# Attention with GpSimd additions of exponentials: block-4 masks placed before the last two additions, one addition in six on VectorE for half of the head groups, later deviations placed after the masks

## What is computed

```python
scores = jnp.einsum('bsnh,btnh->bnst', k, q) / math.sqrt(HEAD_SIZE)
scores = jnp.triu(scores) + -10000.0 * jnp.tril(ones, k=-1)
attn = jax.nn.softmax(scores, axis=2)
out = jnp.einsum('bnkq,bknh->bqnh', attn, v)
out = out.reshape(b, s, NUM_HEADS * HEAD_SIZE)
return out @ Wo + bo
```

## Time and profile before

| | us |
|---|---|
| median of 3 runs (lowest, highest) | 1638.31 (1636.98, 1640.26) |
| the profiled execution | 1638.2 |
| its span in the trace | 1636.3 |
| TensorE busy | 1543.4 |
| VectorE busy | 948.3 |
| ScalarE busy | 796.6 |
| GpSimd busy | 596.5 |
| mean granted share of the TensorE clock | 0.983 |

### The profile page before, as it was taken

One profiled execution on the slowest core, in us unless ns is written; L12 is line 12 of the kernel. 1 busy time (PEld: TensorE's weight loads), 2 busy tenths in 40 slices (PEclk: granted clock), 3 DMA queues, 4 the chain that ended last, 5 costly groups with the idle time before them and its releaser, 6 DMA issues.

```text
span 1636.3 us, 24454 instructions
## 1 busy us (share of the span) xinstructions
PE 1543.4 (94%) x9286; PEld 642.0 (39%) x9288; DVE 948.3 (58%) x1897; ACT 796.6 (49%) x1284; POOL 596.5 (36%) x812
## 2 busy tenths in 40 slices
PE   4899999999999999999998999999999999999997
PEld 2333333333433333343332344444444444444443
DVE  5657766689666878667876333554434343434344
ACT  5356666567666666755786743232222222222222
POOL 4335664677665667746765310020000000000001
PEclk9899999999999999999999999999999999999999
DMA  4221322114421233222355431221111111111000
GB/s 180 91 53 42 83 59 53 53 62 108 122 45 28 85 98 96 73 53 50 107 168 157 129 102 40 58 97 39 45 27 52 26 52 26 52 26 52 0 26 26
DMA packets 113398, 112.26 MB, mean 69 GB/s; under 512 B 69632, under 2 KB 69632, under 8 KB 113024
## 3 DMA queue, kind: packets, MB, share of 16 engines
q1 hardware_dynamic: 113280, 110.69, 24.0%
HBM read 45.37 MB, written 25.17 MB: 43 GB/s over the span
## 4 chain that ended last, share of the span: by engine, by line
PE 72%; POOL 14%; DVE 5%; issue 5%; ACT 3%; POOLq 0%; ACTq 0%; DVEq 0%
PE ps L968 27%; PE ps L889 15%; PE ps L985 13%; PE ps L952 10%; POOL pt L1459 7%; PE ps L926 4%; DVE mcol L1247 2%; POOL rs L1379 1%; PE ps L902 1%; POOL pt L1450 1%; POOL stage L1443 1%; POOL atl L1469 1%; PE ps L910 1%; POOL rs L1376 1%; ACT tq L1074 1%
## 5 line engine op out<-in xcount | busy, mean ns | idle before, releaser
L1101 ACT ACTIVATE pt<-ps,nrm 128x512 f32<-128x512 f32 (+1 forms) x640 | 360.7, 645 | 220.6 <-PE ps L926 202.7
L968 PE MATMUL ps<-x2in,gu 128*128 128x512 f16 x2048 | 462.4, 379 | 0.0
L1247 DVE TENSOR_REDUCE mcol<-ps 128x1 f32<-128x512 f32 (+2 forms) x600 | 305.7, 575 | 149.9 <-PE ps L910 76.6
L968 PEld LDWEIGHTS ps<-x2in,gu 128*128 128x128 f16 x2048 | 200.2, 98 | 241.9 <-ACT sg L1122 0.5
L1376 POOL TENSOR_SCALAR rs<-mv 128x1 f32<-128x1 f32 x120 | 29.9, 249 | 644.7 <-DVE mv L1146 638.2
L1318 DVE SCALAR_TENSOR_TENSOR hf<-ps,usc,sg 128x512 f32<-128x512 f32 x128 | 96.1, 751 | 259.3 <-PE ps L968 245.7
L1127 ACT ACTIVATE hh<-hf 128x512 f16<-128x512 f32 x128 | 80.7, 630 | 258.1 <-DVE hf L1318 244.5
L1459 POOL TENSOR_TENSOR pt<-pt 128x1024 f32<-128x1024 f32 x84 | 203.4, 2442 | 1.8 <-ACT pt L1101 1.8
L952 PE MATMUL ps<-pt,v 128*32 128x512 f32 (+3 forms) x1536 | 189.2, 506 | 1.8 <-DVE rec L1279 1.7
L985 PE MATMUL ps<-wd,hh 128*128 128x512 f16 x496 | 188.0, 379 | 0.0
L985 PE MATMUL ps<-wd,hl 128*128 128x512 f16 x496 | 188.0, 379 | 0.0
(11 more groups left out here) (125 smaller groups left out, 1590.1 us busy)
## 6 DMA issues: line engine op xcount, KB each, us to landing
qpack<-stage SPq DMA_DIRECT2D x192, 64.0 KB, 2.0
kpack<-stage SPq DMA_DIRECT2D x192, 64.0 KB, 2.0
xr<-in_x SPq DMA_DIRECT2D x32, 256.0 KB, 2.8
x1d<-xr SPq DMA_DIRECT2D x32, 256.0 KB, 2.1
x2d<-xh SPq DMA_DIRECT2D x32, 256.0 KB, 2.0
x1in<-x1d SPq DMA_DIRECT2D x8, 1024.0 KB, 6.1
out_x<-yy SPq DMA_DIRECT2D x32, 256.0 KB, 2.0
xin<-in_x SPq DMA_DIRECT2D x24, 256.0 KB, 2.9
```

What stands on the lines that cost most here:

```text
L968: mm = pe.matmul(bk, GU[:, c, m, i * 128:(i + 1) * 128], x2in[:, 1 - k, p, c, :], start=p == 0 and c == 0, stop=p == 1 and c == 3)
L1101: act.activation(Pt[:, PBUF[step], h, off:512], ps[:, BANK[job], off:512], ACT.Exp, scale=esc).then_inc(s_ex, 1)
L1247: mm = dve.tensor_reduce(mcol[:, n % 2, col:col + 1], scores, AX.X, ALU.max)
```

## The change

It does three things, all in the attention.

1. The two masks of block 4 (step 7) are issued by GpSimd ahead of both additions of block 3. Before, they stood between the two.
2. In head groups 2, 3, 6, 7, 10 and 11 the second addition of block 2 is done by VectorE (a new kind of job, "vsum", with its own semaphore), at step 6 behind the maxima and the turned rows of that step and ahead of the maxima of step 7.
3. In steps 0 to 2 only the first deviation stands ahead of the masks; further ones follow the masks. In later steps all stand first, as before.

```diff
--- before.py
+++ after.py
@@ -171,6 +171,13 @@
     return at
 
 
+def sums_of(step):
+
+
+    n, j, kb = step
+    return [("sum", n, j, kb, 0), ("vsum" if kb == 2 and n % 4 >= 2 else "sum", n, j, kb, 2)]
+
+
 def products_of(step, n, s):
 
     if step is None:
@@ -178,8 +185,8 @@
     summed = step[0] < SUMS and step[1] == 1 and step[2] < 4
     out = [] if summed else [("den",) + step]
     out.append(("num",) + step)
-    if summed and step[2] > 0:
-        out += [("sum",) + step + (h,) for h in (0, 2) if h == 0 or s != 7]
+    if summed and step[2] in (1, 2):
+        out += sums_of(step)
     return out + [("den", n, 1, 0)] * (s == NS - 1 and n < SUMS)
 
 
@@ -233,7 +240,9 @@
         for s, (j, kb) in enumerate(STEPS):
             here = rows.get(NS * n + s, [])
             add(("step", n, s))
-            plan += [("dev", DEV_FOR[job[0]], job[1]) for job in here if job[0] in DEV_FOR]
+            devs = [("dev", DEV_FOR[job[0]], job[1]) for job in here if job[0] in DEV_FOR]
+            soon = 1 if s < 3 else len(devs)
+            plan += devs[:soon]
             lot, of = (s + EARLY, n + 1) if s < NS - EARLY else (s + EARLY - NS, n + 2)
             if of < NG:
                 add(("mjob", of, lot))
@@ -243,11 +252,11 @@
             products = products_of(pend, n, s)
             if n < NG - 2:
                 plan += products
-            plan += [("score", n, j, kb, h) for h in range(4)]
+            plan += [("score", n, j, kb, h) for h in range(4)] + devs[soon:]
             if n < NG - 2 and pend is not None and last(*pend[1:]):
                 plan += [("invert",) + pend[:2], ("normalise",) + pend[:2]]
             if s == 7 and n < NG - 2:
-                add(("sum",) + pend + (2,))
+                plan += sums_of(pend)
             if s == NS - EARLY and n + 1 < NG:
                 plan += [("mjoin", n + 1), ("mturn", n + 1)]
             if n >= NG - 2:
@@ -599,7 +608,7 @@
             ("qk", "qh", "tq", "ql", "v", "vw", "mx", "mr", "mj", "mt", "mf", "mg", "ml"))
         s_sc, s_ex, s_dg, s_den, s_num, s_dt, s_iv, s_rc, s_at, s_ah, s_al = (
             sem("s_" + name) for name in ("sc", "ex", "dg", "den", "num", "dt", "iv", "rc", "at", "ah", "al"))
-        s_sum, s_nm, s_ab = sem("s_sum"), sem("s_nm"), sem("s_ab")
+        s_sum, s_vsum, s_nm, s_ab = sem("s_sum"), sem("s_vsum"), sem("s_nm"), sem("s_ab")
         s_wo, s_yt, s_z, s_x1 = (sem("s_" + name) for name in ("wo", "yt", "z", "x1"))
 
         s_g, s_u, s_sg, s_hf, s_hh, s_hl, s_dwn, s_ds, s_y, s_z2, s_fo = (
@@ -629,6 +638,18 @@
             for name in ("act", "pool", "dve"):
                 if name in BY[:jobs]:
                     e.wait_ge(s_cv[name], BY[:jobs].count(name))
+
+        def added(n, kb, h):
+
+            if ("vsum", n, 1, kb, h) in NO:
+                return s_vsum, NO["vsum", n, 1, kb, h]
+            return s_sum, NO["sum", n, 1, kb, h]
+
+        def add_up(engine, job):
+
+            h = job[4]
+            return engine.tensor_tensor(Pt[:, 2, h:h + 2, :], Pt[:, 2, h:h + 2, :],
+                                        Pt[:, PBUF[STEP[job[1:4]]], h:h + 2, :], ALU.add)
 
         def lower_half(no):
 
@@ -1096,7 +1117,7 @@
                         elif before[1] == SUMMED[0]:
                             e.wait_ge(s_den, NO["den", before[0], 1, 0])
                         elif before[1] in SUMMED:
-                            e.wait_ge(s_sum, NO[("sum", before[0]) + STEPS[before[1]] + (h // 2 * 2,)])
+                            e.wait_ge(*added(before[0], STEPS[before[1]][1], h // 2 * 2))
                     e.wait_ge(s_sc, NO[job])
                     act.activation(Pt[:, PBUF[step], h, off:512], ps[:, BANK[job], off:512], ACT.Exp, scale=esc
                                    ).then_inc(s_ex, 1)
@@ -1246,6 +1267,11 @@
                             else:
                                 mm = dve.tensor_reduce(mcol[:, n % 2, col:col + 1], scores, AX.X, ALU.max)
                         mm.then_inc(s_mr, 1)
+                elif kind == "vsum":
+                    n, j, kb, h = a
+                    e.wait_ge(s_ex, NO["score", n, j, kb, h + 1])
+                    e.wait_ge(*added(n, kb - 1, h))
+                    add_up(dve, job).then_inc(s_vsum, 1)
                 elif kind == "mjoin":
                     n = a[0]
                     of_all = mcol[:, n % 2, 0:32].rearrange("p (h q) -> p h q", h=4)[:, :, 4:8]
@@ -1455,9 +1481,8 @@
                     e.wait_ge(s_num, STEP[n, 1, 0])
                     e.wait_ge(s_ex, NO["score", n, j, kb, h + 1])
                     if kb > 1:
-                        e.wait_ge(s_sum, NO["sum", n, j, kb - 1, h])
-                    pool.tensor_tensor(Pt[:, 2, h:h + 2, :], Pt[:, 2, h:h + 2, :], Pt[:, PBUF[STEP[a[:3]]], h:h + 2, :],
-                                       ALU.add).then_inc(s_sum, 1)
+                        e.wait_ge(*added(n, kb - 1, h))
+                    add_up(pool, job).then_inc(s_sum, 1)
                 elif kind == "halve":
                     n, j = a
                     cols = slice(j * 512, (j + 1) * 512)
```

## The result

| | before | after |
|---|---|---|
| median of 6 runs, us (lowest, highest) | 1637.64 (1633.88, 1640.26) | 1643.51 (1642.48, 1644.88) |
| the profiled execution | 1638.2 | 1644.88 |
| its span | 1636.3 | 1643.1 |
| TensorE, VectorE, GpSimd busy | 1543.4, 948.3, 596.5 | 1549.2, 963.8, 584.1 |
| mean granted share of the TensorE clock | 0.983 | 0.978 |

The change is slower: ratio 1.0046, 95% interval 1.0031 to 1.0061, 5.9 us by the medians and 6.7 by the profiled executions. The forecast was 1640.9, with 0.38 on no change and 0.37 on slower; the range, 1630 to 1647, holds the time.

A forecast was written before the change was run, and what follows sets the result against it. TensorE was taken as nearly always occupied in the attention, waiting 26.6 us for GpSimd's masks, with the join late behind them. Gains 6.6, losses 9.3: net 2.7 us slower, 1638.2 + 2.7 = 1640.9, range 1630 to 1647.

The forecast's parts named there:

- The rule of the two engines: Shared SBUF port: a VectorE operation with two SBUF inputs that meets a running GpSimd addition waits for its end.
- the signs named ahead: Right if mask wait under 12 us, join wait 5 to 12, VectorE additions about 3.3 (3, 7, 11) or 1.2 us.
- L1253 short in head groups 5, 9 and 12: Sign of being wrong: the join of the maxima (L1253) is short there, not waiting for a GpSimd addition.
- just too late to slip in between: Head groups 4, 8: join starts about 354.69, additions part at 354.65, so it ends with the second; gain 0.2 each.
- the rival of the slipping join: Join gets between the additions in head groups 2, 4, 5, 8, 9, 12: 7.6 us fall away, 1633.3; chance 0.20.
- 0 and 1: small terms: Edit 1 in head groups 0 and 1: small terms of both signs, taken as 0.
- The step by step account for head groups 3, 7 and 11: VectorE's addition waits for GpSimd's, reductions 3.3 us late, scores wait 1.6; the join also waits; loss 0.9 each.
- the ScalarE rival: The late deviation in head groups 5 and 9 is not absorbed: 3.0 us added, 1643.9; chance 0.11.
- The clock: TensorE's 1.2 GHz level after some waits: 1.0 us counted back in head group 13; head group 6's is within its 1.7.
- the clock, ending slower: TensorE's new waits could each bring a 1.2 GHz stretch, about 1.3 us each; four more give 1646; chance 0.17.
- No change, leaning to slower: The verdict on the whole time: net 2.7 us slower, within the 0.2% (3.3 us) counted as no change.

The follow-up runs named there:

- e4: The changed kernel with the join of the maxima reading one operand (a reduction over pairs) in place of two: 1637.79 us, ratio 1.0009 to the kernel before.
- f2: The kernel before with masks first (edit 1) and the join as a one-operand reduction: 1631.23 us, ratio 0.9959 to the kernel before.
- g3: f4 with VectorE doing the last addition (block 3, heads 2 and 3) in all 14 head groups, behind the join: 1620.79 us, ratio 0.9905 to the kernel before.
- e1: The kernel before with masks first (edit 1) alone: 1643.45 us, ratio 1.0040 to the kernel before.
- f3: The changed kernel with the moved deviations (edit 3) kept for head groups 2, 6 and 10 only: 1641.87 us, ratio 1.0022 to the kernel before.
- f4: The kernel before with masks first, the join as a one-operand reduction, and moved deviations in head groups 2, 6, 10: 1628.38 us, ratio 0.9941.

## Why the prediction came out right

**The rule of the two engines** carried it and holds: in every two-operand case looked at, VectorE waited for the running addition; e4 shows that the hold hangs on the join's second operand, and f2 that the wait for the join is what turned the gain of the masks into a loss. Of the signs named ahead, the waits for masks (11.6 us) and for the join (8.9) and VectorE's additions (3.36 and 1.21 us) came as those of being right. But "L1253 short in head groups 5, 9 and 12", a sign of being wrong, came in 5 and 9 (0.31 and 0.33 us) and not in 12 (2.13).

**Edit 1.** Head groups 2, 12 and 13 came out as worked (+0.8, +1.1, -1.8 for +1.2, +1.2, -1.8). Edit 1 alone gave +2.1 in 12 and -3.0 in 13; there the clock differs too, with a stretch at 0.50 of 6.83 us for 3.41 in 12 and none for one in 13. In 4 and 8 the step "just too late to slip in between" failed: the join came 0.10 us early, not 0.04 late, and the gain was 0.7, within the bounds given. In 5 and 9 it slipped too, where a loss of 1.2 was written; without edits 2 and 3 the join of head group 5 came late, and that head group lost 1.3. So the rival of the slipping join came true in four of its six head groups, and its sum of 7.6 us did not: it counted the wait behind it, for block 5, with 1.0 us in two head groups and with nothing in the others. The step that failed outright is "0 and 1: small terms": head group 1 lost 2.2 us. 1.25 of it stands as the join's wait in the trace after, but it loses as much with the join out of the way (f2). The second addition there ends later than before, and with it the exponentials, masks and products of block 5; and the stretch at 1.2 GHz there is of 6.83 us for 3.41. g3, which takes that second addition off GpSimd, brings head group 1 back to +0.2 and the stretch to 3.41 us. The prediction had this rule of the buffers in its description of the kernel and did not use it in head group 1.

**Edit 2.** The step by step account for head groups 3, 7 and 11 was right to the row: VectorE's addition took 3.36 us (3.3 forecast), TensorE waited 1.28 for banks (1.6), and each group lost 0.8 (0.9). But as a price of edit 2 it was wrong: with the first edit alone they lose the same 0.8, by the join. There the two losses stand in place of one another. In 6 and 10, VectorE's addition waited for nothing and TensorE paid for it at the banks, as written.

**Edit 3.** Head groups 6 and 10 won 1.9 by this edit alone, for 1.7; most of it is a stretch at 1.2 GHz that did not come, which e1 also lacks without this edit. Head groups 5 and 9 lost 1.4 to 1.6 where 0 was taken: the ScalarE rival (3.0 us for both, 0.11) came true. It didn't show in the net of these groups, since the same delay let the join slip through; f3, which takes the delay away, brings the join's wait back.

**The clock** is the other term that failed. 1.0 us was counted back in head group 13. The wait for the mask there did shrink, from 2.68 to 0.60 us, but a stretch at a granted clock of 0.50 still stands there, from 865.60 to 869.01 us (before from 861.36 to 864.77), and the 1.0 did not come. e1, with a wait of 0.86 us in that place, has none, and wins 3.0 in this head group in place of 1.8. Besides, the after trace has two such stretches in head groups 14 and 15, at 896.32 and 927.04 us, where the change does nothing, and loses 2.8 there. e1 and f4 have neither, so these runs do not show them to be a property of the edits. Against the kernel before, the after trace has three stretches of 3.41 us more in the attention (one of them in head group 1) and two fewer (in 6 and 10). Of the 4.0 us between the forecast and the profiled execution, the 1.0 and the 2.8 make 3.8: the rival "the clock, ending slower" explains the miss better than the forecast's other terms do. Before the first score, where all kernels are alike, the first scores of the profiled executions lie up to 3 us apart.

**The sum.** 2.7 was forecast and 5.9 measured, 6.7 between the profiled executions. Of these 6.7, head groups 1 to 13 account for 3.2 (forecast for them 2.7, without the clock 3.7), 0.8 lies ahead of them and 2.8 behind, where the change does nothing. Each kernel has one trace, so how often an execution has these is open. So the forecast of these head groups was near, and partly by luck, as errors cancel: +2.2 in head group 1 against 1.1 less than written in 4 and 8 together and 0.5 less in 5 and 9. "No change, leaning to slower" put the weight a little on the wrong side: the interval, 1.0031 to 1.0061, lies above the 0.2% that it called no change.
